# Layer stage of a graph-transformer layer: each block of divided messages is turned once, VectorE applies the four coefficients to the turned pair out of PSUM, and GpSimd does the division

## The reference

```python
k, q, v = (_decomp(node_feat, node_type, w_comp, w_basis) for each)   # four basis matrices mixed by node type
e  = (q[dst] * (k @ relation_att)[edge_type, src]).sum(-1) * relation_pri[edge_type] * scale
ex = exp(e - segment_max(e, dst)[dst])
agg = segment_sum(ex / segment_sum(ex, dst)[dst] * (v @ relation_msg)[edge_type, src], dst)
out = relu(_decomp(agg, node_type, w_comp_a, w_basis_a) + node_feat @ loop_weight + bias)
return layernorm(x + out)
```

## Time and profile before

| | us |
|---|---|
| median of 3 runs (lowest, highest) | 1361.55 (1359.63, 1362.12) |
| the profiled execution, by the same clock as the runs | 1360.06 |
| its span in the profile | 1358.2 |
| layer stage, 1252 to 1358 on the profile's axis | 106 |
| in it: PE busy, DVE busy, ACT busy, POOL busy | 92.39, 87.32, 53.22, 0.00 |

### The profile page before, as it was taken

The page is one execution under the profiler, slowest core; times in us unless marked ns, Lnnn a source line. Parts: engine busy times, 40 slices in busy tenths (PEclk is TensorE's granted clock), DMA queues, the critical chain, the costliest instruction groups (busy, mean ns, idle before and its releaser), DMA issues.

```text
span 1358.2 us, 30042 instructions
## 1 busy us (share of the span) xinstructions
PE 1059.1 (78%) x6847; PEld 867.1 (64%) x6848; DVE 992.7 (73%) x2879; ACT 801.0 (59%) x2256; POOL 891.3 (66%) x930
## 2 busy tenths in 40 slices
PE   6999999778767776778767688766777776765997
PEld 3545544577666665667766677666667665665997
DVE  6797748687767677767767677776767777776986
ACT  3767757666556465665546566555656555553446
POOL 3575817767777777777777777777777777775000
PEclk9999989887888689986778887887888878888999
DMA  6989785334434444443444344344443434434042
GB/s 180 364 323 367 306 321 163 107 104 117 118 111 116 119 117 116 116 119 109 117 120 117 115 117 117 110 117 118 117 115 117 116 112 117 117 110 133 29 122 83
DMA packets 109636, 194.52 MB, mean 143 GB/s; under 512 B 23353, under 2 KB 75412, under 8 KB 103196
## 3 DMA queue, kind: packets, MB, share of 16 engines
q0 software_dynamic: 41680, 113.71, 29.2%
q1 hardware_dynamic: 65868, 78.84, 16.6%
q10 hardware_dynamic: 1920, 0.36, 0.1%
HBM read 134.15 MB, written 59.48 MB: 143 GB/s over the span
## 4 chain that ended last, share of the span: by engine, by line
POOL 30%; PE 27%; issue 19%; DVE 14%; DVEq 4%; DMA 2%; ACT 2%; POOLq 0%; ACTq 0%; SPq 0%
POOL kv L1350 30%; PE pb L1722 6%; DVE agg L787 3%; PE pb L1889 3%; PE pb L1793 3%; PE pb L1743 3%; PE pb L1835 3%; DVEq L758 3%; PE pb L1987 2%; DMA kv<-table,idx_now 2%; DVE work L738 1%; PE pb L1963 1%; PE pb L1824 1%; DVE kv L488 1%; DVE work L630 1%
## 5 line engine op out<-in xcount | busy, mean ns | idle before, releaser
L1350 POOL DMA_INDIRECT kv<-table,idx_now x832 | 790.6, 950 | 290.1 <-issue 246.8
L787 DVE TENSOR_TENSOR agg<-agg,pb 128x136 f32 x832 | 242.0, 291 | 202.1 <-issue 72.7
L1889 PE MATMUL pb<-work,onehot 128*128 128x136 f32 x1664 | 320.7, 324 | 75.7 <-DVE agg L787 48.2
L1889 PEld LDWEIGHTS pb<-work,onehot 128*128 128x128 f32 x1664 | 266.3, 224 | 96.9 <-issue 74.5
L1835 PE MATMUL pb<-q_all,work 128*128 x1664 | 264.1, 310 | 0.6 <-ACT work L1492 0.4
L1492 ACT ACTIVATE work<-pb 128x512 f32<-128x512 f32 x208 | 123.5, 594 | 234.0 <-PE pb L1824 233.5
L1479 ACT ACTIVATE work<-lane,neg_lane 128x128 f32<-128x128 f32 x800 | 252.9, 389 | 0.0
L1835 PEld LDWEIGHTS pb<-q_all,work 128*128 128x128 f32 x1664 | 240.1, 221 | 7.6 <-issue 6.0
L1824 PE MATMUL pb<-ident,onehot 128*128 128x128 f32 x832 | 155.7, 318 | 57.3 <-ACT onehot L1486 51.9
L630 DVE TENSOR_TENSOR work<-kv,pb 128x512 f32<-128x512 f32 x208 | 142.2, 684 | 74.5 <-DMA kv<-table,idx_now 51.3
L1824 PEld LDWEIGHTS pb<-ident,onehot 128*128 128x128 f32 x832 | 109.7, 162 | 80.7 <-ACT onehot L1486 72.9
(11 more groups left out here) (221 smaller groups left out, 1237.2 us busy)
## 6 DMA issues: line engine op xcount, KB each, us to landing
table<-kv SPq DMA_DIRECT2D x49, 1024.0 KB, 5.6
kv<-table,idx_now POOLq DMA_INDIRECT x832
seg<-item_bias SPq DMA_DIRECT2D x52, 64.0 KB
kv<-base_rows SPq DMA_DIRECT2D x7, 448.0 KB, 4.7
kv<-in_x_dram SPq DMA_DIRECT2D x8, 384.0 KB, 5.6
pair<-in_x_dram SPq DMA_DIRECT2D x24, 128.0 KB
base_rows<-pair SPq DMA_DIRECT2D x24, 128.0 KB
onehot<-in_x_dram SPq DMA_DIRECT2D x7, 384.0 KB
```

The source lines that it names most:

```text
L787: v.tensor_tensor(a, a, PB[banks[i // 2 % len(banks)]][:, (i % 2) * 256:(i % 2) * 256 + W], ALU.add).then_inc(s_added, 1)
L1350: pool.indirect_dma_start(out=kv[:, o:o + 2 * D], out_offset=None, in_=table, in_offset=bass.IndirectOffsetOnAxis(ap=idx_now[par][:, i:i + ...
L1889: mm = t_.matmul(PB[banks[k % len(banks)]][:, u * 256:u * 256 + W], onehot[:, o:o + P], wv[:, b % WR, h * 2 + u, :], start=True, stop=True)
```

## The change

- `part` and the multiplication by the coefficients in `factors` go. GpSimd, behind its last gather, multiplies the chunk's sums by the reciprocal denominators: two instructions for each chunk (2 and 5 blocks, `MADE`), into `an`.
- TensorE turns each block once, not four times, and two blocks (a unit, `UNITS`: blocks 0-1, 2-3, 4-5, 6) go to one PSUM bank.
- ScalarE's `copy_products` goes. VectorE's new `scale(ch, u)` reads the turned unit from PSUM, four times over by a step of zero, multiplies it by the coefficients and writes `anT`: 128x1024 for a pair, 128x512 for the last block.
- Since the data is turned, the coefficients must lie along the columns, equal in all 128 partitions. TensorE turns `ca` at the start of the groups, ScalarE copies it out, and SyncE writes it to DRAM as `coef_rows`. In the layer stage SyncE loads it for each chunk, repeated to all partitions: 1024 KB for blocks 0 to 3 and 768 KB for blocks 4 to 6.
- The order on VectorE, TensorE, ScalarE and SyncE is written anew. `scale(ch+1, 0)` directly follows `scale(ch, 3)`, and `residual` is cut in two.

```diff
+            def scale(ch, u):
+                c0, c1 = UNITS[u]
+                n = ch * len(UNITS) + u
+                if n >= 2:
+                    last = UNITS[(u - 2) % len(UNITS)][1]
+                    dve.wait_ge(s_block_multiplied, (ch - (u < 2)) * CB + last)
+                dve.wait_ge(s_coefs_loaded[ch % 2][c0 >= HALF], (ch // 2 + 1) * 16)
+                dve.wait_ge(s_products_turned, n + 1)
+                turned = PB[TURN_BANKS[n % 2]][:, 0:(c1 - c0) * P].rearrange("p (c n) -> p c n", c=c1 - c0)
+                v.tensor_tensor(anT[:, n % 2, 0:c1 - c0, :, :],
+                                turned.unsqueeze(2).broadcast_to([P, c1 - c0, NB, P]),
+                                coef_of(ch, c0, c1), ALU.mult).then_inc(s_scaled, 1)
...
             for ch in range(2, 5):
+                scale(ch, 0)
                 weigh_last(2 * ch - 2)
-                residual(ch - 1, (ch - 1) % 2)
+                residual(ch - 1, (ch - 1) % 2, 0)
+                scale(ch, 1)
                 weigh_last(2 * ch - 1)
                 batch(2 * ch - 3)
-                inverse(ch - 1)
+                residual(ch - 1, (ch - 1) % 2, 1)
                 batch(2 * ch - 2)
                 factors(ch + 1)
-                part(ch + 1, 0)
-                part(ch + 1, 1)
+                scale(ch, 2)
+                inverse(ch - 1)
+                scale(ch, 3)
...
+            def load_coefs(ch, c0, c1):
+                r = (ch * CB + c0) * NB
+                many = (c1 - c0) * NB
+                sp.dma_start(coef_of(ch, c0, c1).rearrange("p c b n -> p (c b) n"),
+                             coef_rows[r:r + many, :].rearrange("(a r) n -> a r n", a=1).broadcast_to([P, many, P]))\
+                    .then_inc(s_coefs_loaded[ch % 2][c0 >= HALF], 16)
+            def more_coefs(ch):
+                sp.wait_ge(s_scaled, (ch - 1) * len(UNITS))
+                load_coefs(ch, 0, HALF)
+                load_coefs(ch, HALF, CB)
...
+            for ch in range(CHUNKS):
+                ag = agg[:, ch * CB * W:(ch + 1) * CB * W].rearrange("p (c w) -> p c w", c=CB)
+                pool.wait_ge(s_factors, ch * V3 + V3)
+                after(pool, s_products_turned, ch - 1, len(UNITS), 0)
+                for c0, c1 in MADE:
+                    g_.tensor_tensor(an[ch % 2][:, c0 * D:c1 * D].rearrange("p (c h k) -> p c h k", c=c1 - c0, h=H),
+                                     ag[:, c0:c1, 0:D].rearrange("p c (h k) -> p c h k", h=H),
+                                     rden[ch % 2][:, c0:c1, :].unsqueeze(3).broadcast_to([P, c1 - c0, H, DK]),
+                                     ALU.mult).then_inc(s_products_made, 1)
...
+            def turn_products(ch, u):
+                for k, (m0, _) in enumerate(MADE):
+                    if c0 == m0:
+                        pe.wait_ge(s_products_made, ch * len(MADE) + k + 1)
+                if n >= 2:
+                    pe.wait_ge(s_scaled, n - 1)
...
                 for c in range(CB):
+                    if c % 2 == 0 and c + 1 < CB:
+                        turn_products(ch, c // 2 + 1)
+                    elif c + 1 == CB and ch + 1 < CHUNKS:
+                        turn_products(ch + 1, 0)
                     multiply(ch, c)
                     for k in halves.get(c, ()):
                         sums(GROUPS - 1, 1, k)
...
             stage3(1, {2: (0, 1), 5: (2, 3)})
             stage3(2, {2: (4, 5), 5: (6, 7)})
-            stage3(3, {3: (8, 9), 6: (10, 11)})
-            stage3(4, {3: (12, 13), 6: (14, 15)})
+            stage3(3, {2: (8, 9), 5: (10, 11)})
+            stage3(4, {2: (12, 13), 5: (14, 15)})
```

More of the change, by code:

```diff
@@ L219, in graph_transformer_layer @@
         yo = (s3.take(CN), prod.rearrange("p r u d -> p (r u d)")[:, 0:CN])
[L220 to L222 removed]
+        an = [s3.take(CN) for _ in range(2)]
         stats = s3.take(CB * 6).rearrange("p (c k) -> p c k", c=CB)
@@ L227, in graph_transformer_layer, with take_coefs @@
         eps = s3.take(1)
-        assert s3.at <= G * 2 * D and NB * CN <= min(BLOCKS * D, G * P)
-        anb = [Space(t, NB * CN).take(NB * CN).rearrange("p (b n) -> p b n", b=NB) for t in (q_all, onehot)]
+        assert s3.at <= G * 2 * D
+        q3 = Space(q_all, BLOCKS * D)
+        h3 = Space(onehot, G * P)
+        HALF = 4
+        def take_coefs(space, blocks):
+            return space.take(blocks * NB * P).rearrange("p (c b n) -> p c b n", c=blocks, b=NB)
+        even_coefs = take_coefs(q3, CB)
+        first_coefs, odd_coefs = take_coefs(h3, HALF), take_coefs(h3, HALF)
+        anT = q3.take(2 * 2 * NB * P).rearrange("p (r c b n) -> p r c b n", r=2, c=2, b=NB)
+        rden = [q3.take(CB * H).rearrange("p (c h) -> p c h", c=CB) for _ in range(2)]
         last_weights = fwd
@@ L373, in graph_transformer_layer, with coef_of @@
         OUT_BANKS = ((3, 1), (6, 7))
[L376 to L380, removed]
+        MADE = ((0, 2), (2, CB))
+        UNITS = ((0, 2), (2, 4), (4, 6), (6, CB))
+        def coef_of(ch, c0, c1):
+            if ch % 2:
+                return (first_coefs if c0 >= HALF else odd_coefs)[:, c0 % HALF:c0 % HALF + c1 - c0, :, :]
+            return (first_coefs if ch == 0 and c0 < HALF else even_coefs)[:, c0:c1, :, :]
         def final_items(ch):
@@ L875, in part @@
[L875 to L909, removed]
+                chained(v.tensor_scalar(rden[ch % 2], ag[:, :, D:W], 1e-30, None, ALU.max), s_factors, ch * V3, 1)
@@ new lines, in residual @@
+            def residual(ch, par, h):
+                c0, c1 = ((0, 4), (4, CB))[h]
+                if h == 0:
+                    after(dve, s_normalised, ch - 1, CB, 0)
+                dve.wait_ge(s_block_multiplied, ch * CB + c1)
+                v.scalar_tensor_tensor(y[par][:, c0 * D:c1 * D], out_of(ch, c0, c1 - c0),
+                                       0.0, x3[par][:, c0 * D:c1 * D], ALU.max, ALU.add)\
+                    .then_inc(s_residual, 1)
+                dve.wait_ge(s_residual, ch * 2 + h + 1)
+                for c in range(c0, c1):
+                    v.bn_stats(stats[:, c, :], y[par][:, c * D:(c + 1) * D]).then_inc(s_stats, 1)
+                if h == 1:
+                    dve.wait_ge(s_stats, ch * CB + CB)
+                    after(dve, s_shift, ch, 1, 0)
+                    hold_apart(dve)
+                    for c in range(CB):
+                        v.bn_aggr(mv[:, c, :], stats[:, c, :]).then_inc(s_mean_var, 1)
@@ L956, in _ @@
             v.memset(eps, EPS)
+            factors(0)
             late[0]()
             late[1]()
-            factors(0)
-            part(0, 0)
             scans()
@@ L963, in _ @@
             late[3]()
+            scale(0, 0)
             carried()
-            part(0, 1)
+            scale(0, 1)
             late[4]()
@@ L1169, in _ @@
             load(1, 1)
+            sp.wait_ge(s_item_sums, (GROUPS - 2) * 2 * NBATCH + HALF * NB // 2)
+            load_coefs(0, 0, HALF)
             store_pair(PAIRS - 1)
             sp.wait_ge(s_base_stored, 16 * PAIRS)
-            with sp.Fori(0, CHUNKS // 2 - 1) as it:
-                load(it * 2 + 2, 0)
-                store(it * 2, 0)
-                load(it * 2 + 3, 1)
-                store(it * 2 + 1, 1)
-            load(CHUNKS - 1, 0)
+            sp.wait_ge(s_edge_queries, GROUPS * NBATCH)
+            load_coefs(0, HALF, CB)
+            sp.wait_ge(s_item_sums, (GROUPS - 1) * 2 * NBATCH)
+            load_coefs(1, 0, HALF)
+            sp.wait_ge(s_scaled, HALF // 2)
+            load_coefs(1, HALF, CB)
+            for ch in range(2, CHUNKS):
+                more_coefs(ch)
+                if ch >= 3:
+                    store(ch - 3, (ch - 3) % 2)
+                load(ch, ch % 2)
             for ch in range(CHUNKS - 3, CHUNKS - 1):
```

146 lines of the change are left out of this document (70 added, 76 removed).

## The result

The changed kernel takes 1368.48 us (median of 7 runs, 1367.40 to 1374.28) against 1360.77 (7 runs, 1355.94 to 1362.12) for the kernel before. The ratio is 1.0074, 95% interval 1.0062 to 1.0087. It is worked out from all the runs and not from the two medians: their means, 1369.68 and 1359.66, give 1.0074 too, the medians 1.0057. So the change is slower, by 10.1 us on the 1361.55 that the prediction started from, where 10.5 were forecast; by the medians it is 7.7 us. The profiled execution took 1368.05, its span 1366.3.

The account below looks back on a forecast made before the run. VectorE was taken to set the pace of chunks 1 to 4, TensorE of the last two. Terms of +6.0 us and 5 for the clock made +11 on 1360.06; with 1.5 for the median, 1372 (range 1368 to 1378).

Parts of the forecast that it names:

- rival (a): Layer stage: stalls as forecast, but the clock stays at 2.4 GHz or falls once; +4 to +7 us, 1367; chance 0.20.
- stalls at `scale(2..5, 0)`: VectorE waits for the next chunk's turned pair, queued on TensorE behind products and sums; four at 2.7 us, 10.8.
- the clock: TensorE's clock falls to 1.2 GHz after its new pauses in the layer stage; 0 to 15.5 us, taken as 5.
- stall at `scale(6, 0)`: The same VectorE wait for the turned pair, without sums ahead of it on TensorE; 1.8 us.
- start, `scale(1, 0)`: VectorE waits for the first coefficients of chunk 1, whose buffer is freed late; 2.4 us.
- waits at the end: VectorE's 4.6 us of waits in the last chunks shrink to 1.1, left for ScalarE's root; -3.5 us.
- work of VectorE: Dropping `part` and the coefficient product (-30.0, -3.0) and adding `scale` (28.1) leaves VectorE 4.9 us less.
- scattered waits: VectorE's small waits for TensorE in the batches go; -0.6 us.
- rival (e): Every pause brings the slow clock for all TensorE work behind it; +21.5 us, 1383; chance 0.06.
- Rival (c): Coefficients come late, so each chunk waits for its loads; +18 us and more, 1380 or later; chance 0.06.
- Rival (b): TensorE sets the layer stage's pace, so fewer turns make it faster; -8 to -9 us, 1353; chance 0.12.
- Rival (d): VectorE's stalls are half as long; 1361 to 1364; chance 0.13.

Follow-up runs that it names:

- `fill_pause`: Changed kernel, with TensorE repeating the base product of block 4 twelve times before its wait for scale(ch, 2) in chunks 1 to 6; ratio 1.0054 to the kernel before.
- `clear_divide_on_vector`: `spread_scales` with inverse ahead of factors, half the residual ahead of weigh_last, x loaded ahead of the store, division on VectorE; 1362.04 us, 1.0022 of the kernel before.
- `spread_scales`: Changed kernel, with scale(ch, 0) behind weigh_last and half the residual, and scale(ch, 2) right behind the first batch; ratio 0.9990 to the kernel before.
- `two_chunks_of_coefs`: Changed kernel without the coefficient loads for chunks 2 to 6, which reuse those of chunks 0 and 1; ratio 1.0086 to the kernel before.
- `sums_behind_turn`: Changed kernel, with the second pair of the last group's sums issued after block 6, behind the turn, in chunks 1 to 4; ratio 1.0060 to the kernel before.
- `spread_load_first`: `spread_scales` with only the load of x moved ahead of the store on SyncE's queue; ratio 1.0000 to the kernel before.
- the last four runs: The last four of twelve experiment kernels, run beside a kernel before that took 2021.15 and 2022.37 us.

## Why the prediction was right

The ratio applied to the 1361.55 gives 1371.6 (1370.0 to 1373.4); 1372 was forecast. The measured median, 1368.48, is nearer to rival (a)'s 1367, so the total alone would not tell the two apart; the steps do. By its steps, in microseconds, with the stage of the profiled executions:

| term | predicted | measured |
|---|---|---|
| stalls at `scale(2..5, 0)`, four at 2.7 and the clock 5 | 15.8 | 15.4: four at 2.31 are 9.2, and the clock 6.1 |
| stall at `scale(6, 0)` | 1.8 | 1.74 |
| start, `scale(1, 0)` | 2.4 | 0.81 |
| waits at the end | -3.5 | -3.9 (4.6 to 0.65) |
| work of VectorE | -4.9 | -2.2 |
| scattered waits | -0.6 | -1.4, what is left over |
| sum | +11.0 | +10.4 |

**The stall** was the mechanism, in the predicted place and with the predicted releaser. PE's way from the end of `scale(L, 2)` to the turned pair was priced at 3.6, and at full clock, from `scale(1, 2)` to `scale(2, 0)`, it took 1282.54 - (1277.71 + 1.22) = 3.6. The size was off by 0.4 on VectorE's side: behind `scale(L, 2)` it had not 0.9 but 1296.20 - 1294.91 = 1.3 us to do, since L927 took 0.55 and not 0.17. What was held there would otherwise have been waited, so in those places the held step cost nothing.

**The clock** fell after pauses of 3.48, 3.82 and 3.47 us and not after those of 2.30 and 2.41: three of five, and they cost 6.1 us, where 5 were taken as a third of the upper bound of 15.5. That this came so near is luck: nothing in the working says a third. That rival (a), with no fall or one, was wrong is shown by the granted clock of 0.50 behind three pauses and by `fill_pause`; rival (e), a fall at every pause, by the 2.31 at `scale(2, 0)`. The named rule of the Trainium skill (TensorE: Matmul & The Clock Gate, "HAM oscillation"), waits between bursts that bring the slow clock back, agrees for the three longer pauses of the kernel after and not for those of 2.30 and 2.41. The earlier trace rows had suggested that 2.43 is enough. Over the other runs the pauses with a fall and those without overlap widely. In `fill_pause` 1.87 us had the slow clock behind it, and in `clear_divide_on_vector` 3.37 us had not; the eight records behind it take 1.16, and PEclk is 1.00:

```profile
1281.79 1.16 PE L2029 MATMUL pb<-Ba,q_all 128*128 128x128 f32 x8 [3.37 <-DVE q_all L904]
```

The length of one pause alone does not tell, so the 5 us of the forecast were a good guess for this execution and could not be worked out.

**The work of VectorE.** The prices 1.14 and 0.60 held: 1293.68 to 1294.82 is 1.14, and the groups are 1216 and 685 ns. What was missed is in the sentence that costs GpSimd's division at nothing. The division itself is hidden (1.85 us for a chunk; 2.1 were expected), but it holds VectorE: 6 x (426 - 167) = 1.6 and 956 - 286 = 0.7 us, which is 2.2 of the 2.7 that the work came out too dear. I had looked at what waits for GpSimd and not at what runs beside it. In the result it was small because the stalls swallowed most of it; in `spread_scales`, without the stalls, it showed.

**The start** was dearer in the forecast than on the chip: the load of 1024 KB lands after 4.7 us, and the 0.81 ends with PE's turn, not with a load. (In `fill_pause` it did end with one, 1.18 us.) Rival (c), coefficients late in each chunk, is dismissed by `two_chunks_of_coefs`. Rival (b), TensorE's pace, is dismissed by the 19.9 us that PE waits. Rival (d) needed stalls of half the size. The errors of the start (-1.6) and of the work (+2.7) went against each other, so the sum is somewhat better than its parts, and that is luck too.

## What to carry to other kernels

When a copy on a free engine is replaced by a step in a full engine's queue, two in-order queues now wait for each other: write down for each new wait what stands behind it, and put independent steps ahead of it before counting what the edit saves. Here the same work took 112, 104, 101 or 95 us for the stage by the order of VectorE's queue (the last with one moved load beside), the clock that followed from it included. Work given to GpSimd is cheap if VectorE's neighbours in time read PSUM, and taxes each step with two SBUF inputs that starts while it runs.

## What the runs showed of the hardware

- A VectorE instruction with two SBUF inputs that starts while a GpSimd `tensor_tensor` runs is held until that ends: 0.17 became 0.55 and 1.09 (ends within 0.03 us of each other), and 0.29 became 0.96 (0.16 us behind GpSimd's end), while PSUM-and-SBUF instructions kept their 1.22. The other way round, GpSimd's division behind such an instruction took 2.36 and not 1.85.
- A 128x1024 product on VectorE, one input from PSUM four times over by a step of zero, costs its successor 1.14, and one of 128x512 0.60; the latter takes 685 ns, and the 128x512 from PSUM of the earlier trace rows takes 681.
- TensorE's granted clock was 0.50 for 3 to 6 us after pauses of 3.5 to 3.8 us between bursts, and it did not fall where these three pauses were filled with products. Over all runs a pause of 1.87 us had a fall behind it and one of 3.37 had none.
- Not settled: what decides at pauses between 1.9 and 3.4 us, why the start of the stage ran at the low clock for 15 us and not 7 to 8 in `sums_behind_turn` and `spread_load_first`, and why the groups took 660 us longer beside the last four runs.
